# Graph attention rounds: the gather adds onto receivers' rows laid in its buffer

## The reference

```python
xn = layernorm(x)
h = rmsnorm(xn) * rms_w @ W_down                   # 1250 x 256
src, dst = edges plus one loop per node
xl, xr = (h @ Wl), (h @ Wr)                        # 4 heads of 64
msg = xl[src] + xr[dst]
e = einsum(leaky_relu(msg, 0.2), att)              # per edge and head
p = exp(e - segment_max(e, dst)[dst])
out = segment_sum(p / segment_sum(p, dst)[dst] * xl[src], dst)
gnn = out @ W_up
mix = (q k^T * scale) v @ Wo + bo                  # linear, no softmax; q, k, v from xn
x = x + gnn + mix
x = x + nvfp4_ffn(layernorm(x))                    # weights and rows rounded to FP4 in blocks of 16
```

## Time and profile before

| what | value |
|---|---|
| median of 3 runs | 1125.42 us (1121.11 to 1128.18) |
| the profiled execution | 1124.86 us |
| its span | 1122.3 us |
| PE busy | 970.0 us (86%) |
| DVE busy | 956.2 us (85%) |
| ACT busy | 528.2 us (47%) |
| POOL busy | 616.1 us (55%) |

### The profile page before, as it was taken

How to read it: one execution, slowest core, us unless ns; L and a number is a source line. 1 busy time by engine, 2 the same in 40 slices (tenths; PEclk the granted TensorE clock), 3 DMA queues, 4 the chain that set the end, 5 groups by cost and what they waited for, 6 DMA issues and landing times.

```text
span 1122.3 us, 10318 instructions
## 1 busy us (share of the span) xinstructions
PE 970.0 (86%) x2998; PEld 465.6 (41%) x2998; DVE 956.2 (85%) x1078; ACT 528.2 (47%) x1901; POOL 616.1 (55%) x657
## 2 busy tenths in 40 slices
PE   0798999999999998999999999998999947566754
PEld 0675544444574343444344444443444423222321
DVE  6989648492999999999999999899997387888795
ACT  0123213311666677667878878767776121111111
POOL 2323327446666666676777777767762264444332
PEclk9899999999969999999999999998999967867788
DMA  8104051244343432553355333573320100000001
GB/s 255 76 1 119 10 181 34 51 142 139 100 155 80 155 83 77 158 160 98 87 156 171 84 82 91 208 280 81 91 79 22 61 1 0 38 19 19 20 37 52
DMA packets 59462, 105.30 MB, mean 94 GB/s; under 512 B 24631, under 2 KB 32468, under 8 KB 59130
## 3 DMA queue, kind: packets, MB, share of 16 engines
q0 software_dynamic: 18560, 50.70, 16.2%
q1 hardware_dynamic: 40842, 53.92, 14.4%
HBM read 92.30 MB, written 12.45 MB: 93 GB/s over the span
## 4 chain that ended last, share of the span: by engine, by line
DVE 48%; PE 32%; issue 10%; POOL 4%; SPq 2%; ACT 1%; DMA 1%; POOLq 0%; DVEq 0%; ACTq 0%
PE acc L715 25%; DVE acc_sb L1428 11%; DVE z L1558 7%; DVE round_mem L1556 7%; DVE round_mem L1419 4%; PE acc L888 3%; DVE round_mem L1174 3%; DVE round_mem L1175 2%; DVE round_mem L1173 2%; POOL round_mem L666 2%; PE acc L886 2%; POOL round_mem L490 1%; DVE round_mem L1172 1%; DVE big_b L1496 1%; DVE big_b L1372 1%
## 5 line engine op out<-in xcount | busy, mean ns | idle before, releaser
L666 POOL DMA_INDIRECT round_mem<-msg_table,idx x352 | 338.0, 960 | 99.9 <-issue 88.8
L1109 ACT ACTIVATE round_mem<-round_mem,pz 128x66 f32<-128x66 f32 x1408 | 345.1, 336 | 2.0
L715 PE MATMUL acc<-wslot,big_a 128*128 128x512 f32 x512 | 225.1, 600 | 4.4 <-issue 2.1
L1428 DVE TENSOR_REDUCE acc_sb<-round_mem 128x264 f32<-128x1848 f32 (+1 forms) x62 | 206.2, 3326 | 5.9 <-ACT round_mem L1109 3.8
L490 POOL TENSOR_TENSOR round_mem<-round_mem 128x1024 bf16<-128x1024 bf16 (+3 forms) x52 | 85.6, 1653 | 132.6 <-DVE round_mem L1176 87.7
L715 PEld LDWEIGHTS acc<-wslot,big_a 128*128 128x128 f32 x512 | 97.9, 193 | 127.5 <-issue 123.1
L715 PE MATMUL acc<-big_a,xhat_t 128*128 128x512 f32 x320 | 139.9, 600 | 6.5 <-ACT xhat_t L1039 5.0
L1102 ACT ACTIVATE pz<-z 128x7 f32<-128x7 f32 (+1 forms) x248 | 55.5, 296 | 148.3 <-DVE z L1565 105.7
L1419 DVE TENSOR_TENSOR round_mem<-round_mem,tp 128x1536 f32<-128x1536 f32 (+1 forms) x62 | 103.4, 1668 | 25.3 <-issue 19.8
L715 PE MATMUL acc<-wslot,big_b 128*128 128x512 f32 x256 | 113.1, 601 | 8.9 <-DVE big_a L1375 6.3
L715 PE MATMUL acc<-big_b,wslot 128*128 128x512 f32 x256 | 110.0, 592 | 0.0
(11 more groups left out here) (195 smaller groups left out, 1159.7 us busy)
## 6 DMA issues: line engine op xcount, KB each, us to landing
big_b<-in_x SPq DMA_DIRECT2D x18, 512.0 KB, 10.9
round_mem<-msg_table,idx POOLq DMA_INDIRECT x352
out_x<-big_b SPq DMA_DIRECT2D x9, 512.0 KB
wslot<-in_wv_t SPq DMA_DIRECT2D x2, 2048.0 KB
wslot<-in_wk_t SPq DMA_DIRECT2D x2, 2048.0 KB
wslot<-in_wo_t SPq DMA_DIRECT2D x2, 2048.0 KB
wslot<-in_wq SPq DMA_DIRECT2D x2, 2048.0 KB
wslot<-in_gate_w SPq DMA_DIRECT2D x1, 2048.0 KB
```

The costliest lines, as they stand in the source:

```text
L666: pool.indirect_dma_start(xg[g % 4][:, j, :], None, msg_table, bass.IndirectOffsetOnAxis(idx[:, c, j0 + j:j0 + j + 1], 0)).then_inc(xg_in[ ...
L715: mm = nc.tensor.matmul(o(acc[:, n % 4, :]), a, b, start=first, stop=last)
L1109: ins = nc.scalar.activation(xg[g % 4][:, j, cols], xg[g % 4][:, j, cols], ACT.Copy, scale=pz[:, g % 2, j, h:h + 1])
L1428: nc.vector.tensor_reduce(acc_sb[:, c, :], xg[g % 4][:, 0:n + 1, :].rearrange("p j f -> p f j"), AX.X, ALU.add).then_inc(sum_done, 1)
```

## The change

Receivers' rows are kept in the same form as senders' rows (66 values a head, `ROW` wide, the last column 0 instead of 1). ACT lays the receiver's row in every slot of a round's buffer (`lay_receivers`), and the gather adds the senders' rows onto them by the DMA's add. `add_receiver`, `complete` and the receivers' copies in PSUM go. DVE subtracts the least score itself, so that ACT's exponential is one instruction. At a chunk's end the receiver's row is subtracted from the result. Unused slots fetch row NOBODY (1279), whose linear score is 1e30 (`far_col`). The first gather goes ahead of the scaling of weight piece 10, the piece behind `p` 4 is turned behind `p` 3, and round 0 has its intermediate values in the fourth gather buffer, so that only round 1 waits for the stores. The planner's constants change. The diff's core:

```diff
-ROUND_0_AT, ROUND_STEP = 286.0, 9.6
+ROUND_0_AT, ROUND_STEP = 270.0, 8.4
-                ("gram", 15): 8, ("p", 1): 9, ("p", 2): 10, ("p", 4): 11}
+                ("gram", 15): 8, ("p", 1): 9, ("p", 2): 10, ("p", 3): 11}
+NOBODY = NP - 1
+        xr_table = nc.dram_tensor("xr_table", (NP, ROW), F32, kind="Internal").ap()
+        scores_of = [(round_mem[0:NC, a:a + R * HID].rearrange("p (j h d) -> p j h d", j=R, d=DH)) for a in (3 * (R + 1) * ROW, m0)]
-        early = {index_of["p", i]: 273.0 + 3 * i for i in range(3)}
+        early = {index_of["p", i]: 257.0 + 2 * i for i in range(3)}
...
 GpSimd
+            def gather(g):
+                c, j0, n, _, _ = ROUNDS[g]
+                pool.wait_ge(receivers_laid, g + 1)
+                for j in range(n):
+                    pool.indirect_dma_start(xg[g % 4][:, j, :], None, msg_table,
+                                            bass.IndirectOffsetOnAxis(idx[:, c, j0 + j:j0 + j + 1], 0),
+                                            compute_op=ALU.add).then_inc(xg_in[g % 4], 16)
+            step(nc.gpsimd.memset(far_col[:], 0.0))
+            nc.gpsimd.affine_select(out=far_col[:], in_=far_col[:], compare_op=ALU.is_gt, fill=FAR, base=LAST_ROWS,
+                                    pattern=[[0, 1]], channel_multiplier=-1).then_inc(pool_const, 1)
                     if q < 4 * n + 3:
                         enter_piece(q + 1)
+                    if q == 10:
+                        pool.wait_ge(idx_done, 1)
+                        pool.wait_ge(table_out, 16)
+                        gather(0)
                     leave_piece(q)
...
-            for g, (c, j0, n, _, _) in enumerate(ROUNDS):
-                if g == 1:
-                    pool.wait_ge(wq_tp, 12)
+            for g in range(1, LAST + 1):
                 if g >= 3:
                     rescale(g - 3)
-                for j in range(n):
-                    pool.indirect_dma_start(xg[g % 4][:, j, :], None, msg_table,
-                                            bass.IndirectOffsetOnAxis(idx[:, c, j0 + j:j0 + j + 1], 0)).then_inc(xg_in[g % 4], 16)
-                if g >= 1:
-                    complete(g - 1)
+                gather(g)
                 if g - 5 in LAST_OF:
                     send_attention(LAST_OF.index(g - 5))
...
 ScalarE
+            def lay_receivers(g):
+                c, _, n, _, _ = ROUNDS[g]
+                if g == 3:
+                    act.wait_ge(z_done, 1)
+                if g >= 4:
+                    act.wait_ge(sum_done, g - 3)
+                nc.scalar.copy(xg[g % 4][:, 0:n, :], xr_sb[:, c, :].unsqueeze(1).to_broadcast([NC, n, ROW])).then_inc(receivers_laid, 1)
             for i in range(16):
+                if i == 2:
+                    act.wait_ge(xr_in, 16 * C)
+                    nc.scalar.copy(att_ps, att_sb[0:NC]).then_inc(att_done, 1)
+                    lay_receivers(0)
                 if ("p", i) in TURNED_AFTER:
                     piece(TURNED_AFTER["p", i])
...
+            for g in range(1, 3):
+                lay_receivers(g)
             for g, (c, _, slots, first, _) in enumerate(ROUNDS):
                 for n in due("act", g):
                     take(n)
                 act.wait_ge(z_done, g + 1)
-                for h in range(H):
-                    ins = nc.scalar.activation(pz[:, g % 2, 0:slots + 1, h], z[:, g % 3, 0:slots + 1, h], ACT.Exp, scale=-1.0,
-                                               bias=z[:, (g + 1) % 3, top_slot(g + 1), h:h + 1])
-                ins.then_inc(e_done, 1)
+                nc.scalar.activation(pz[:, g % 2, 0:slots + 1, :], z[:, g % 3, 0:slots + 1, :], ACT.Exp, scale=-1.0).then_inc(e_done, 1)
...
                 ins.then_inc(mul_done, 1)
+                if g + 3 <= LAST:
+                    lay_receivers(g + 3)
...
 VectorE
+            nc.vector.memset(xr_sb[:].rearrange("p c (h d) -> p (c h) d", d=HR)[:, :, ONE], 0.0).then_inc(xr_zeroed, 1)
...
-                        step(nc.vector.tensor_tensor(unused[:], slot_b, deg_b, ALU.is_gt))
+                        step(nc.vector.tensor_tensor(t_idx, t_idx, node_b, ALU.add))
+                        step(nc.vector.tensor_tensor(lt_idx, slot_b, deg_b, ALU.is_gt))
-                        nc.vector.tensor_tensor(idx[:], t_idx, node_b, ALU.add).then_inc(idx_done, 1)
+                        nc.vector.scalar_tensor_tensor(idx[:], lt_idx, float(NOBODY), t_idx, ALU.mult, ALU.max).then_inc(idx_done, 1)
...
 close, at the end of a chunk
+                    step(nc.vector.tensor_tensor(heads[:, :, 0:DH], heads[:, :, 0:DH],
+                                                 den.unsqueeze(2).to_broadcast([NC, H, DH]), ALU.mult))
                     nc.vector.tensor_tensor(gnn_out[c].rearrange("p (h d) -> p h d", d=DH), heads[:, :, 0:DH],
-                                            den.unsqueeze(2).to_broadcast([NC, H, DH]), ALU.mult).then_inc(gnn_norm, 1)
+                                            xr_sb[:, c, :].rearrange("p (h d) -> p h d", d=HR)[:, :, 0:DH], ALU.subtract).then_inc(gnn_norm, 1)
...
 the rounds
+                m4 = scores_of[min(g, 1)]
+                if g == 1:
+                    for w in wt_out:
+                        dve.wait_ge(w, 16 * 6)
+                dve.wait_ge(xg_in[g % 4], 16 * GATHERED[g])
+                step(nc.vector.scalar_tensor_tensor(m4[:, 0:slots], xg[g % 4][:, 0:slots, :].rearrange("p j (h d) -> p j h d", d=HR)[:, :, :, 0:DH],
+                                                    0.0, att_ps.unsqueeze(1).to_broadcast([NC, slots, H, DH]), ALU.max, ALU.mult))
-                step(nc.vector.scalar_tensor_tensor(m_flat[:, 0:slots], m_flat[:, 0:slots], 0.0,
-                                                    att_ps.unsqueeze(1).to_broadcast([NC, slots, HID]), ALU.max, ALU.mult))
...
-                nc.vector.tensor_reduce(top, zz[:, 0:slots + 1].rearrange("p j h -> p h j"), AX.X, ALU.min).then_inc(z_done, 1)
-                dve.wait_ge(z_done, g + 1)
-                if g < LAST:
-                    step(add_receiver(g + 1))
+                step(nc.vector.tensor_reduce(top, zz[:, 0:slots + 1].rearrange("p j h -> p h j"), AX.X, ALU.min))
+                nc.vector.tensor_tensor(zz[:, 0:slots + 1], zz[:, 0:slots + 1], top.unsqueeze(1).to_broadcast([NC, slots + 1, H]),
+                                        ALU.subtract).then_inc(z_done, 1)
                 if g >= 1:
                     close(g - 1)
```

More of the change, by code:

```diff
@@ L164, in gps_layer @@
         idx_junk = idx[:].rearrange("p c j -> p (c j)")[:, 0:NP // 4].bitcast(BF16)
-        unused = sb("unused", [NC, C, SLOTS], U8)
+        far_col = sb("far_col", [NC, 1])
         att_sb = sb("att_sb", [P, H, DH])
@@ L288, in gps_layer @@
         gnn_out = [xr_sb[:, c, 0:HID] for c in range(C)]
-        xr_ps = [tp[0:NC, c % 2, 0:HID] for c in range(C)]
-        att_ps = tpb[0:NC, 0, 0:2 * HID].bitcast(F32)
+        att_ps = tp[0:NC, 0, 0:HID].rearrange("p (h d) -> p h d", d=DH)
         gnn_nat = [acc_sb[:, c, 0:HID] for c in range(C)]
@@ L621, in add_bias @@
                                             ALU.add).then_inc(base_done, 1)
-            def complete(g):
-                c, j0, n, first, _ = ROUNDS[g]
-                if first:
-                    if g >= 1:
-                        pool.wait_ge(lin_done, g)
-                    cap = CAPS[c]
-                    step(nc.gpsimd.tensor_scalar(beside[:, 0:cap, :], unused[:, c, 0:cap].unsqueeze(2).to_broadcast([NC, cap, H]), FAR, None, ALU.mult))
-                    step(nc.gpsimd.tensor_tensor(beside[:, 0:cap, :], beside[:, 0:cap, :],
-                                                 xr_sb[:, c, DH:H * MR:MR].unsqueeze(1).to_broadcast([NC, cap, H]), ALU.add))
-                pool.wait_ge(xg_in[g % 4], 16 * GATHERED[g])
-                lin = xg[g % 4][:, 0:n, DH:ROW:HR]
-                nc.gpsimd.tensor_tensor(lin, lin, beside[:, j0:j0 + n, :], ALU.add).then_inc(lin_done, 1)
             def send_attention(c):
@@ L1025, in take @@
                         b = 2 * H * c
-                        nc.scalar.activation(acc_sb[:, c, DH:ROW:HR], a[0:NC, b:b + H], ACT.Copy, scale=rrms[:, c:c + 1])
-                        ins = nc.scalar.activation(xr_sb[:, c, DH:H * MR:MR], a[0:NC, b + H:b + 2 * H], ACT.Copy,
+                        nc.scalar.activation(acc_sb[:, c, DH:ROW:HR], a[0:NC, b:b + H], ACT.Identity, scale=rrms[:, c:c + 1],
+                                             bias=far_col[:, 0:1] if c == C - 1 else 0.0)
+                        ins = nc.scalar.activation(xr_sb[:, c, DH:ROW:HR], a[0:NC, b + H:b + 2 * H], ACT.Copy,
                                                    scale=rrms[:, c:c + 1])
@@ L1098, in _ @@
                 act.wait_ge(z_done, g + 1)
-                if first and 1 <= c < C - 1:
-                    show_receivers(c + 1)
-                for h in range(H):
-                    ins = nc.scalar.activation(pz[:, g % 2, 0:slots + 1, h], z[:, g % 3, 0:slots + 1, h], ACT.Exp, scale=-1.0,
```

(29 more changed lines are left out.)

59 lines of the change are left out of this document (22 added, 37 removed).

## The result

The changed kernel takes 1305.75 us (median of four, 1303.32 to 1310.94) against 1125.83 for the kernel before: a ratio of 1.161, 95% interval 1.156 to 1.167. It is 180 us slower. The forecast was 1122, its range ended at 1150.

A forecast was written before the change was run, and what follows sets the result against it. DVE, ACT and POOL rounds were taken to set ACT's copies, and the copies PE. From 1124.86 us, 3.8 gained and 0.6 added gave 1121.7, or 1122.2 on the median; forecast 1122 us, range 1106 to 1150.

The forecast's parts named there:

- The descriptors are built on the same index and row sizes, so I take the 0.96 rows: POOL's adding gathers in the rounds: claimed to cost 0.96 us each like plain ones, starting 1.26 us apart.
- rival C: Rounds 2 to 55: the adding gather costs POOL more; 1184 us if gathers start 1.50 us apart; chance 0.24.
- the rival's own sum: POOL's time over rounds 2 to 55: 308 times the distance between gather starts, plus 30 and 11 us.
- 137.4 + 1 in my working: PE's end of products: 20 groups of 6.87 us after the copy, 137.4 us, plus 1 for the clock.
- Rounds set the time of a copy and the copy sets PE: PE's products: copies stand in planned rounds, so PE waits for ACT's copy; base group 0 starts at 735.7 us.
- 1.35 chosen: ACT's laying of receivers in a six-slot round: 1.35 us, within 1.2 to 1.9, no row showing it.
- The 1.5 us for a landing: The start, gather 1: data land about 1.5 us after the last issue, at about 280 us.
- mutual waiting: Rounds 28 to 55: DVE, ACT and POOL wait for each other in a ring; 5 us added, 224 in all.
- B, the looser ring: Rounds 28 to 55 at 7.7 us without mutual wait, round 2 at 286: 1109 us; chance 0.28.
- one dear gather, 0.7 us: First gathers, moved beside DVE's weight rounding: one of six takes 0.7 us more, bounds 0 and 4.1.
- the rule: Moved gathers: VectorE instructions with two SBUF inputs contend with GpSimd's SBUF reads; two dear gathers, start 0.7 us later.
- the break-even (here 1.31 us): POOL's distance between gather starts at which the products end at 877.3 us, even with before; 1.26 was assumed.

The follow-up runs named there:

- experiment 1: The changed kernel with plain gathers that replace the laid row instead of adding to it: 1163.34 us, ratio 1.037 to the kernel before.
- experiment 3: The kernel before with the adding alone, its gathers from round 4 on adding onto the buffer's old rows: 1249.88 us.
- experiment 6: The changed kernel with one constant changed, the planner's round step 12.0 us instead of 8.4: 1234.70 us, ratio 1.099 to the kernel before.
- experiment 9: The changed kernel with plain gathers of half a row, 528 bytes instead of 1056: 1131.75 us, ratio 1.005 to the kernel before.

## Why the prediction was wrong

**The step that failed** is "The descriptors are built on the same index and row sizes, so I take the 0.96 rows". The term was 308 gathers at a pitch of 1.26; it measured 1.86, which is 185 us more on POOL. That lies inside the bounds I had written down (1.26 to 1.95), nearly at the upper one. I chose the value by a likeness of descriptors, although no row showed an indirect transfer that adds, and gave its rival C a chance of 0.24 and worked it out to 1.50 and no further. Experiments 1 and 3 show the term alone: 142 us out of the changed kernel, 128 into the kernel before.

**The mechanism around it was right.** With the measured pitch the rival's own sum is 308 x 1.86 + 41 = 614 us. Round 2's first pass stood at 305.6 instead of 290, behind gathers of 1.86 each. 305 + 614 = 919 is where round 56 should start; ACT copied the last t2 group at 921.3. From there 20 groups took 139.6 us (137.4 + 1 in my working), and the tail 242 again. "Rounds set the time of a copy and the copy sets PE" held as well: experiment 6 gave back 71 us by moving copies and nothing else.

**The rest of the sum.** DVE's add line is gone, the subtract takes 0.19 us and the exponential 0.23. Laying took 1.51 us for six slots, against 1.35 chosen and 1.9 at most. With the adding and the standstills out of the way (experiment 9), round 56's copy was done at 746.8 where I had 735.7, and the time was 1131.75 where I had 1122. Of these 11 us about 6 are a later start: ACT took round 2's scores at 300.2, 294 by my working. The 1.5 us for a landing, an estimate without a row, has a part in this: in experiment 9 the last gather of round 1 ended on POOL at 283.40, and DVE went on at 286.53, 3.1 us later. The other 5 are mutual waiting, for which I had added 5 us already: between 300 and 745 POOL waited 23.8 us for layings and DVE 16.7 for rescales. So, as far as half rows can stand for whole ones, B, the looser ring, would have been wrong too, and with this plan the change would have gained nothing had the adding been free.

**What no step had.** With plain gathers there are 31.6 us more between whole and half rows (1163.3 against 1131.75), with 28.6 us before ACT's multiplies in the one against 2.0 in the other, and a `p0` of 40.1 us against 23.0. No row of the kernel before shows such standstills, and I could not have priced them.

**The moved gathers.** I took one dear gather, 0.7 us, and two by the rule. In the changed kernel they took 1.54 to 2.21 us each, and PE's turn of piece 10 came at 265.66 for 259.3. Experiment 1 shows them plain, and DVE's steps beside the first two:

```profile
250.75 1.26 POOL L506 DMA_INDIRECT round_mem<-msg_table,idx  x1 [3.87 <-DVE idx L1400]
252.31 1.65 POOL L506 DMA_INDIRECT round_mem<-msg_table,idx  x1 [0.30 <-issue]
254.26 0.95 POOL L506 DMA_INDIRECT round_mem<-msg_table,idx  x1 [0.30 <-issue]
255.52 1.44 POOL L506 DMA_INDIRECT round_mem<-msg_table,idx  x1 [0.30 <-issue]
257.27 1.66 POOL L506 DMA_INDIRECT round_mem<-msg_table,idx  x1 [0.30 <-issue]
...
251.19 0.69 DVE L1170 TENSOR_SCALAR round_mem<-round_mem 128x1024 f32<-128x1024 f32 x1
251.91 1.23 DVE L1171 SCALAR_TENSOR_TENSOR wslot<-round_mem,wslot 128x1024 f32<-128x1024 f32 x1
253.17 1.22 DVE L1172 SCALAR_TENSOR_TENSOR round_mem<-round_mem,wslot 128x1024 bf16<-128x1024 f32 x1
```

Four of six are dear, by 2.2 us in all, where I had 0.7 and the rule 1.4. The two of 1.65 and 1.66 lie beside DVE's rounding steps with two inputs in SBUF, which ran from 251.91 to 254.39 and from 256.88 to 259.37. In this the trace agrees with the Trainium skill ("SBUF — State Buffer", section "Who interferes with whom"); the 1.26 and 1.44 ran for most of their time beside DVE's TENSOR_SCALAR steps of 0.69 us (250.47 to 251.88 and 255.43 to 256.85). The same section of the Trainium skill names `tensor_scalar` too among the operations that can contend, which my working left out; the two gathers of 0.95 ran beside such steps of 0.43 us, in bf16, and weren't longer.

## What to carry to other kernels

An operation that no row shows is not priced by its nearest look-alike: where both bounds are written down and the break-even (here 1.31 us) lies near the lower one, the upper bound belongs in the range. Moving work off the longest engine pays only if each other engine has room for its own share of it in the same round; count the engine that issues descriptors as one of them. Where copies are written into fixed rounds, a round longer than planned is paid twice, by the rounds and by the engine whose results wait in them; and if two chains end together, as at 874 and 878 here, both must be cut before the time moves.

## What was not expected of the hardware

- An indirect gather that adds in SBUF cost POOL 1.555 us for 0.960, with 128 packets of one row each for 32 packets of four rows. It cost the same at half the bytes (1.554 us). At half the rows the adding still cost 0.51 us, for 0.595 at all rows.
- A stop of PE is paid again behind it: 16 matmuls took 9.29 us after the stop of 10.93 and 10.03 after that of 9.70, for 6.87 in a full run; the granted clock of the stretch from 284 to 545 was 0.85 in the changed kernel and 0.95 in the kernel before.
- ACT and TensorE can stand still in steps of 0.7 us with no releaser in the profile: 14.4 to 44.1 us before ACT's multiplies in the five kernels with plain gathers of whole rows in the changed order, 2.0 in the kernel before, with adding gathers, and with half rows. TensorE's `p0` took 37.2 to 43.6 us in the same five and 22.1 to 25.1 in all others. DVE shows 15.6 us without a releaser before its folds in experiment 1 and none in the kernel before. Neither the laying, nor the bytes, nor the far row is the cause by itself, and the plan of the copies changes them (28.6 to 15.8 us); what the cause is stays open.
